# Second attention of a three-stage kernel: scores with the keys on partitions, maxima taken from separate masked scores

## The reference, cut to what matters

```
x = x + xattn(layernorm(x), ctx)      # 16 heads of 16, 4096 keys per batch from ctx
x = x + attn(layernorm(x))            # 16 heads of 16, 256 keys per batch, |i - j| <= 32 only
x = x + ffn(layernorm(x))             # router, 2 of 16 banks per token, 256 -> 1024 -> 256
```

```
qkv = x @ w_qkv + b_qkv
scores = einsum('bhqd,bhkd->bhqk', q, k) / 4 + mask     # mask: 0 within 32 tokens, else -inf
attn = softmax(scores)
out = einsum('bhqk,bhkd->bhqd', attn, v) @ w_out + b_out
```

## Time and profile before

| | us |
|---|---|
| median of 3 runs | 1396.68 (1395.20 to 1401.56) |
| the profiled execution, its own time | 1402.28 |
| its span in the profile | 1400.5 |
| from the copy after the last weighing of the first attention (L964) to the last sum of the second (L1176) | 938.5 to 1116.1 |

### The profile page before, as it was taken

One profiled execution on the slowest core, in us unless ns is written; L12 is line 12 of the kernel. 1 busy time (PEld: TensorE's weight loads), 2 busy tenths in 40 slices (PEclk: granted clock), 3 DMA queues, 4 the chain that ended last, 5 costly groups with the idle time before them and its releaser, 6 DMA issues.

```text
span 1400.5 us, 29968 instructions
## 1 busy us (share of the span) xinstructions
PE 1291.0 (92%) x12251; PEld 800.7 (57%) x12251; DVE 919.1 (66%) x1727; ACT 750.7 (54%) x1043; POOL 270.3 (19%) x244
## 2 busy tenths in 40 slices
PE   7789999999999999999999999988998529999996
PEld 4444444555444455444455544437777429999995
DVE  5778888676888776888767788536677652222224
ACT  4236777676777766777667677844465301111110
POOL 5130212111121211121111111101500011222210
PEclk8989999999999999999999999998999959999998
DMA  7553574533364444357334443100000049999952
GB/s 214 84 74 47 77 162 65 77 54 46 52 134 99 67 69 60 52 105 129 53 52 68 62 61 47 48 8 0 2 1 17 0 158 408 363 333 324 323 195 102
DMA packets 48360, 150.22 MB, mean 107 GB/s; under 512 B 17040, under 2 KB 21152, under 8 KB 40288
## 3 DMA queue, kind: packets, MB, share of 16 engines
q1 hardware_dynamic: 43664, 135.60, 42.1%
q0 software_dynamic: 2976, 8.13, 1.8%
q10 hardware_dynamic: 1584, 4.59, 0.8%
HBM read 88.63 MB, written 6.16 MB: 68 GB/s over the span
## 4 chain that ended last, share of the span: by engine, by line
PE 84%; DVE 8%; ACT 4%; issue 2%; DMA 1%; SPq 0%; DVEq 0%; ACTq 0%
PE psum L546 20%; PE psum L528 14%; PE psum L506 10%; PE psum L844 8%; PE psum L856 8%; PE psum L427 7%; PE psum L444 6%; ACT wts L919 2%; PE psum L715 2%; DVE o_norm L1158 2%; DVE part_max L1116 1%; PE psum L733 1%; PE psum L627 1%; DVE biased L1254 1%; PE psum L574 1%
## 5 line engine op out<-in xcount | busy, mean ns | idle before, releaser
L1116 DVE TENSOR_REDUCE part_max<-psum 128x1 f32<-128x512 f32 x1024 | 656.2, 686 | 180.5 <-PE psum L506 179.1
L919 ACT ACTIVATE wts<-psum 128x1024 f32<-128x1024 f32 x512 | 516.1, 1024 | 96.2 <-PE psum L528 95.2
L546 PE MATMUL psum<-wts,vals 128*17 128x256 f32 x4096 | 319.3, 387 | 0.0
L528 PEld LDWEIGHTS psum<-queries,keys 51*128 51x128 f32 x2048 | 158.3, 186 | 201.9 <-issue 142.6
L528 PE MATMUL psum<-queries,keys 51*128 51x256 f32 x2048 | 260.9, 333 | 7.9 <-ACT wts L919 7.0
L506 PE MATMUL psum<-keys,queries 51*128 51x512 f32 x1024 | 229.9, 444 | 24.9 <-DVE part_max L1116 14.9
L1056 ACT ACTIVATE hid<-psum,b1s 128x128 f32<-128x128 f32 x124 | 35.4, 369 | 207.6 <-PE psum L844 207.6
L546 PEld LDWEIGHTS psum<-wts,vals 128*17 128x17 f32 x4096 | 69.7, 95 | 121.5 <-issue 98.4
L506 PEld LDWEIGHTS psum<-keys,queries 51*128 51x128 f32 x1024 | 97.9, 186 | 42.2 <-DVE part_max L1116 28.3
L844 PE MATMUL psum<-xTt,w1s 128*128 128x128 f32 x992 | 117.7, 278 | 0.2 <-DVE xTt L1436 0.2
L844 PEld LDWEIGHTS psum<-xTt,w1s 128*128 128x128 f32 x992 | 115.1, 194 | 0.6 <-issue 0.6
(11 more groups left out here) (188 smaller groups left out, 1009.3 us busy)
## 6 DMA issues: line engine op xcount, KB each, us to landing
keys<-key_high SPq DMA_DIRECT2D x256, 128.0 KB, 4.4
w1s<-in_W SPq DMA_DIRECT2D x31, 1024.0 KB
w2s<-in_W SPq DMA_DIRECT2D x31, 1024.0 KB
keys<-key_low SPq DMA_DIRECT2D x128, 128.0 KB, 6.1
ctx_in<-in_ctxT SPq DMA_DIRECT2D x12, 768.0 KB, 7.9
ctx_in<-in_ctxT ACTq DMA_DIRECT2D x4, 768.0 KB, 10.7
queries<-query_high SPq DMA_DIRECT2D x64, 32.0 KB, 4.6
queries<-query_low SPq DMA_DIRECT2D x32, 32.0 KB, 4.8
```

The lines of the kernel that those rows point to most:

```text
L528: m = e.matmul(bank(S_BANKS[S_NO["s", n] % 2] + i)[:, hh * SEQ:(hh + 1) * SEQ], keys[64 * i:64 * i + STK, hh, c, at:at + P], queries[g % 3 ...
L546: i = e.matmul(bank(O_BANK)[32 * j:32 * j + VW, 0:SEQ], vals[:, t, h * VW:(h + 1) * VW], wts[n % NW][:, j * SEQ:(j + 1) * SEQ], start=(t = ...
L919: i = e.activation(wts[n % NW], s_bank(job, 2), ACT.Exp, scale=QSCALE)
L1116: e.reduce_max(part_max[g % 2][:, hq, c:c + 1], bank(M_BANKS[n % 3]), AX_X).then_inc(dve_max, 1)
```

## The change

A pair p (one batch, four heads) becomes the unit of the loop; the loop runs over i = 1 to 20 and holds several pairs at different stages. Heads of a group are taken by parity (heads 0, 2, 4, 6 of a half or 1, 3, 5, 7), so that each of the four lies in its own 32 rows with its neighbour set to zero. There are only two masked copies of the queries, written as the projection leaves PSUM (`q_parity`), and no `mask_half`.

- PE `max2(p, qt)`: scores with the queries on partitions, for the maxima only. The mask is put into PSUM first, as a bf16 product of the identity and the mask; then four heads of 32 contraction rows, two at a time in two banks (4 and 5), with a wait between the two twos. DVE takes minus the maximum straight from PSUM.
- DVE `pieces2`: splits it into three bf16 pieces. PE `neg2` turns them (bank 6), ACT `neg_rows` copies them to SBUF as bf16 rows.
- PE `scores2(p)`: mask, scores with the keys on partitions (four heads of 32 rows in banks 0 to 3), and rows of minus the maximum through a weight of ones. ACT `exps` takes exp of 128 x 640 from PSUM, twice a pair; the result is used by `weigh2` as it stands.
- The normalization: ACT copies the spread sums (`sums2`), DVE takes the reciprocal, POOL multiplies and adds the bias.
- The first two `max2` are issued in steps 509 and 511 of the first attention. The projection of the last batch of the first attention is made in one piece at i = 1, instead of twelve instructions at step 512 and four after `last_norm`.
- The second half of transposed rows, queries, keys and values comes in three lumps, at i = 4, 5 and 6, through banks 0 to 3; the copies are shared between ACT and DVE.
- Host-side layouts of w_out, b_v and hmask follow the order by parity.

The diff, cut to its core:

```
-                if n == STEPS:
-                    e.wait_ge(dve_early, 10)
-                    e.wait_ge(pool_norm, LAST)
-                    project_some(wo, range(NG - 1), M_BANKS)
+                if n in FIRST_MAX2:                       # (STEPS - 3, STEPS - 1)
+                    max2(0, FIRST_MAX2.index(n))
...
+            def max2(p, qt):                              # PE
+                ...
+                    e.wait_ge(dve_m2, 2 * p + qt)
+                for odd in range(2):
+                    for i in range(2):
+                        e.matmul(bank(W_BANKS[i])[:, odd * WIN:(odd + 1) * WIN], identb, wmaskb[:, qt],
+                                 start=True, stop=False)
+                    if odd:
+                        e.wait_ge(pe_even2, 2 * p + qt + 1)
+                    for i in range(2):
+                        r = slice(32 * (2 * i + odd), 32 * (2 * i + odd) + 32)
+                        t = e.matmul(bank(W_BANKS[i])[:, odd * WIN:(odd + 1) * WIN], q2[r, par, m, tok:tok + P],
+                                     k2[r, m, keys_at:keys_at + WIN], start=False, stop=True)
+                    t.then_inc((pe_even2, pe_m2)[odd], 1)
+            def neg2(p):                                  # PE
+                e.wait_ge(dve_neg2, p + 1)
+                e.wait_ge(x_free, X_NO["neg2", p])
+                for qt in range(2):
+                    t = e.matmul(bank(X_BANK)[:, qt * P:(qt + 1) * P], neg_parts2[p % 2][:, qt]..., identb, ...)
+            def scores2(p):                               # PE
+                    e.wait_ge(act_w2, 2 * p)
+                ...
+                for h in range(GH):
+                    e.matmul(bank(h)[:, 0:2 * WIN], identb, wmaskb..., start=True, stop=False)
+                for kt in range(2):
+                    for h in range(GH):
+                        e.matmul(bank(h)[:, kt * WIN:(kt + 1) * WIN], k2[r, m, tok:tok + P], q2[r, par, m, at:at + WIN], ...)
+                for kt in range(2):
+                    for h in range(GH):
+                        t = e.matmul(bank(h)[:, kt * WIN:(kt + 1) * WIN], ones2[r], neg_rows2[p % 2][r, at:at + WIN], ...)
+            def weigh2(p, kt):                            # PE
+                for lo, hi, first in (((0, WIN, True),), ((SEQ - WIN, WIN, False), (WIN, SEQ, True)))[kt]:
+                    for h in range(GH):
+                        t = e.matmul(o[32 * h:32 * h + VW, lo:hi], vals2[...], w[:, h, at:at + hi - lo], ...)
...
+            for i in range(1, PAIRS + 5):                 # PE
+                max2(i, 0); weigh2(i - 3, 0); scores2(i - 2); max2(i, 1)
+                weigh2(i - 3, 1); norm2(i - 4); neg2(i - 1)
+                if i == 1: last_project()
+                if i == 4: ... turn_half(1, k, bank(k))
+                if i == 5: ... qk_half(1, m, bank(m))
+                if i == 6: ... v_tile2(TT // 2 + t, bank(t))
+                if i in (8, 12, 16): project2((i - 8) // NG)
+                if i == PAIRS: turn3(0)
+                if i == PAIRS + 1: logits(0); turn3(1)
+                if i == PAIRS + 2: logits(1)
+            for i in range(1, PAIRS + 5):                 # ACT
+                exps(i - 2); ocopy2(i - 3); sums2(i - 4); neg_rows(i - 1)
+                for n in {4: ..., 5: ..., 6: ...}.get(i, ()): half(n)
+            for i in range(1, PAIRS + 5):                 # DVE
+                max2(i, 0); reciprocals2(i - 5); max2(i, 1); pieces2(i)
+                if i == 1: add_last(); statistics(last)
+                if i == 2: root(last); apply(xn2, last, dve_rows2)
+                if i == 5: ... q_parity(1, m, bank(m), dve_half)
+                ...
```

More of the change, by code:

```diff
@@ L601, in project2, with norm2 @@
+            def norm2(p):
+                e.wait_ge(act_ocopy2, p + 1)
+                e.wait_ge(x_free, X_NO["norm2", p])
+                e.matmul(bank(X_BANK)[:, 0:SEQ], lsel, o_raw2[p % 2], start=True, stop=True).then_inc(pe_norm2, 1)
             def project2(b):
[L602 removed]
+                e.wait_ge(pool_norm2, NG * (b + 1))
                 e.wait_ge(x_free, X_NO["out2", b])
@@ L608, in project2, with last_project @@
                 i.then_inc(pe_out2, 1)
+            def last_project():
+                e.wait_ge(pool_norm, LAST)
+                e.wait_ge(dve_lastnorm, 1)
+                e.wait_ge(x_free, X_NO["out"])
+                for qt in range(BT):
+                    for hg in range(NG):
+                        i = e.matmul(bank(X_BANK)[:, qt * EMB:(qt + 1) * EMB], o_norm[:, hg, qt * P:(qt + 1) * P],
+                                     wo[:, hg], start=(hg == 0), stop=(hg == NG - 1))
+                i.then_inc(pe_lastout, 1)
             def project_some(w, groups, to):
@@ new lines, in _ @@
+            for i in range(1, PAIRS + 5):
+                if i < PAIRS:
+                    max2(i, 0)
+                if 0 <= i - 3 < PAIRS:
+                    weigh2(i - 3, 0)
+                if 0 <= i - 2 < PAIRS:
+                    scores2(i - 2)
+                if i < PAIRS:
+                    max2(i, 1)
+                if 0 <= i - 3 < PAIRS:
+                    weigh2(i - 3, 1)
+                if 0 <= i - 4 < PAIRS:
+                    norm2(i - 4)
+                if i - 1 < PAIRS:
+                    neg2(i - 1)
+                if i == 1:
+                    last_project()
+                if i == 4:
+                    e.wait_ge(act_w2, 2 * (i - 1))
+                    for k in range(KE):
+                        turn_half(1, k, bank(k)).then_inc(pe_half, 1)
+                if i == 5:
+                    e.wait_ge(act_w2, 2 * (i - 1))
+                    for m in range(2 * KE):
+                        qk_half(1, m, bank(m)).then_inc(pe_half, 1)
+                if i == 6:
+                    e.wait_ge(act_w2, 2 * (i - 1))
+                    for t in range(TT // 2):
+                        v_tile2(TT // 2 + t, bank(t)).then_inc(pe_half, 1)
+                if i >= 8 and i % NG == 0 and (i - 8) // NG < BATCH - 1:
+                    project2((i - 8) // NG)
+                if i == PAIRS:
+                    turn3(0)
+                if i == PAIRS + 1:
+                    logits(0)
+                    turn3(1)
+                if i == PAIRS + 2:
+                    logits(1)
```

472 lines of the change are left out of this document (224 added, 248 removed).

## The result

The changed kernel takes 1381.5 us (median; 1375.8 to 1383.2) beside 1397.5 of the kernel before on the same chip: a ratio of 0.9875, interval 0.9838 to 0.9912. It is faster by 16 us between the medians and by 1.25% by the ratio, and the interval is clear of no change. Forecast was 1372, faster, in a range of 1352 to 1398. Sign and range hold; the gain is 16 us instead of 25. Its profiled execution took 1381.6 by its own time, 20.7 less than that of before.

The account below looks back on a forecast made before the run. PE's instruction stream was taken to set the pace, 6.45 us a pair; stage terms 0.4 + 22.9 + 77.4 + 12.2 + 8.2 + 1 + 30.3 = 152.4 us against 177.6 gave 1377 profiled, 1372 median; range 1352 to 1398.

Parts of the forecast that it names:

- TensorE's stream sets the pace, and how long it is for a pair: Steady iteration: PE's instructions for a pair take 5.9 us, plus waits at neg2, a period of 6.45; before 7.3.
- Its terms: PE's stream per pair: max2 twice 2.8 us, scores2 1.55, weigh2 1.0, norm2 0.43, neg2 0.11.
- A change of division: Switching how PE's array is divided between products: 0.25 us each, ends 0.20 and about 0.45; 12 a pair, 192 in all.
- The rival of dear changes: Changes of the array's division cost more: gain gone at 0.38 us each, 1405 at 0.42; chance 0.13.
- Four sets of rows abreast: 32-row products on PE overlap four at a time, 0.033 us each; rival of overlap two by two, 1383, chance 0.14.
- The end of the first attention at nothing: Before the stage: two max2 add 2.8 us, the leaving L614 block saves 2.86, so no net effect.
- The start, 22.9 and 0.4: Stage's beginning, i = 1 to 3: 22.9 us after a copy of 0.4.
- The twelve iterations with lumps and two projections: i = 4 to 15: iterations 77.4 us, lumps 12.2, two projections 8.2, VectorE's statistics 1.
- The end, 30.3: From i = 16 to the last addition: third projection done at 8.9 us, POOL at 26.9, last projection and addition at 30.3.
- The offset: Whole kernel: 1377 for the profiled execution, lowered to 1372 because the profiled execution before stood 5.6 above its median.
- the clock: Rival: PE at 1.2 GHz in a third of the stage, +20 to +45 us, 1405 to 1420; chance 0.04 shared with no overlap.
- the copies out of PSUM gave nothing by going: Stage: removed copies of the turned weights lie beside PE already, so the sum credits their removal with nothing.

Follow-up runs that it names:

- run 1: Changed kernel with neg2 of the pair before moved right behind its first max2, and its ScalarE copy to the iteration's head; 1376.4 us, ratio 0.981.
- run 2: Changed kernel with three 128-row products of zeros a pair added in scores2, so six more changes of the array's division a pair; 1393.6 us, ratio 0.9945.
- run 3: The control: changed kernel with the same added products of zeros in scores2, but through 32 rows, so no added change of division; 1381.5 us, ratio 0.9864.
- run 6: Changed kernel with the mask products of max2 left out, maxima over all 160 keys; 1375.9 us, ratio 0.9839.
- run 5: Changed kernel with filler products only, in TensorE's long waits at i = 1, before neg2 of i = 16 and before the last projection; 1375.4 us, ratio 0.9838.
- run 7: Changed kernel with one mask product of 320 columns per bank in max2 instead of one of 160 per group; 1382.8 us, ratio 0.9898.
- run 9: run 8 plus filler products in TensorE's remaining waits, at i = 3, 4 and 16 to 18, behind the third projection and router products; 1364.7 us, ratio 0.9755.
- run 8: Changed kernel with neg2 early, twelve instructions of the first attention's last projection moved into the gap at i = 1, and some fillers; 1370.8 us, ratio 0.9791.
- 10: run 9 with the mask products of max2 left out as well, fillers kept; 1354.6 us, ratio 0.9683.
- 11: Same kernel as 10 (neg2 early, projection in the gap, no max2 masks) without any filler; 1358.7 us, ratio 0.9716.

## Why the prediction was right, and where it was off

- **TensorE's stream sets the pace, and how long it is for a pair**: right. 6.56 for 6.45, and run 1 confirms the wait of 0.57 by removing it: 6.02. That the sum came so near is in part luck, as the next point shows.
- **Its terms**: right only in their sums. A change of division was taken as 0.25, by the distance to a product that follows another; it is 0.11 by itself (runs 2 and 3, and run 6) for changes between 32-row and 128-row products, the only pairing tested. Three errors made up for it. In max2 the wait between the even and the odd groups was to fall into a change; it is 0.34 and longer than one. In scores2 the four masks were set at 0.40, though the price of 0.067 for 160 columns makes them 0.53, and 0.65 lies between the first of the sixteen products and the next block, not 0.53. And a max2 by the prediction's own prices (masks 0.13 and products 0.13, both twice, and four changes of 0.25) is 1.52, not 1.4. With these two sums put right the period would have come out at about 6.8. The rival of dear changes, given a chance of 0.13, is refuted: it needed 0.38.
- **Four sets of rows abreast**: right. In run 2 each half of the products, eight instructions, takes 0.49 to the next block with a change in it; at 0.033 each they are 0.27, and two by two 0.53 without any change. In the control eight take 0.38 (1023.19 to 1023.57) and in the changed kernel sixteen 0.65, so eight more add 0.27. By the Trainium skill's factor of 3.07 ("TensorE: Matmul & The Clock Gate", Measured speedup vs the span model), which is stated for 512 columns, the sixteen would take 0.69, an estimate; the 0.65 with what stands behind the last is under it.
- **The end of the first attention at nothing**: the copy is at 938.99, before at 938.53. That neither confirms nor refutes it, since kernels with the same instructions reach that copy anywhere from 931.9 to 939.0.
- **The start, 22.9 and 0.4**: this step failed. max2(4, 0) starts 25.25 behind the copy, 1.95 late. The wait behind last_norm was in the sum, 2.2 us; that everything behind it, max2(1, 1) and sixteen projections, ran at 1.2 GHz was not: 1.0 and 1.5 us, a little of it given back by VectorE's work alongside. Run 5, with that wait filled, confirms it: 22.65 us, 2.6 less, and 0.65 under the sum's 23.3.
- **The twelve iterations with lumps and two projections**: 98.74 by the trace (964.24 to 1062.98), 98.8 by the sum, but by errors that cancel. Twelve periods of 6.56 are 78.7, 1.3 over; the three lumps took 11.3 for 12.2 and the two projections 8.5 for 8.2; of the 1 us for VectorE's statistics 0.2 is left.
- **The end, 30.3**: the same step again. The last projection starts 26.84 behind max2's place in i = 16 (1062.98 to 1089.82), for 26.9, but this is luck. The third projection ended 11.2 behind that place and not 8.9, with 1.7 of the 2.3 us by its low clock (5.38 for 3.69), and the profile's chain of work that ended last runs through the whole of it. What made up for it is that the rest up to L708 took 15.65 us, for 18.0. Then L708, behind its 3.4 us of waiting, took 5.45, and with the addition 5.98 (to 1095.80) instead of 3.4. Of these 2.6 us the clock is 1.8; at full clock in run 5 the same two take 4.14, so 3.4 was 0.7 too low by itself.
- **The offset**: the sum gave 1377 for the profiled execution, and 1381.6 was measured, 4.5 over. The stage has 4.4 of them (156.8 for 152.4): 1.95 at the start and 2.6 at the end. The other 5 us of the miss in the median are the 5.6 that I took off for the profiled execution of before. That was a run at a clock of 0.965, while runs of before in the later sets reach 0.972, and there was no reason for the changed kernel's profiled run to stand off its own median; it did not.
- **Rivals**: the clock stood there with 0.04 together with another, as a third of the stage at 1.2 GHz. It should have been a term of the sum: small in this kernel (7.8 us by 156.8 at 0.95, about what the stage before has, 177.6 at 0.95), and up to 29 us in those that take work off TensorE (run 6; but run 2, which adds work, has 25). The price written there slips too: 20 to 45 us on 1372 are 1392 to 1417, not 1405 to 1420. That the copies out of PSUM gave nothing by going is not shown. No run takes them alone away, and in the kernel before TensorE did wait for them between 950 and 1120, ten times and 9.0 us in all, 0.19 at a time in the dense part (at 1029.89 and at 1037.21) and 4.0 once:

```profile
PE psum L728 <- ACT wTa L1018: 9.0, 10, 4.0
```

So of the 25 us expected in the stage 20.8 came in the profiled executions. Nothing was lost in the steady part and 4.5 us went at both ends. The low clock cost more than that there, 2.6 us at the start (run 5), 1.7 and 1.8 at the two projections of the end; smaller terms of the sum that were too high hid the rest. The main step that went wrong is one: everything behind a long wait of TensorE was priced at the full clock. It made the gain smaller, not the direction wrong.

## What to carry to other kernels

Work the steady iteration out by distances between starts and the round trip of one bank, and it can come out to 2%, as here, partly by errors that cancel: check each term, and not only the sum. Then ask of every wait of TensorE what the granted clock does behind it. Behind 2.1 to 3.4 us it fell every time here, behind 0.3 to 1 us in some executions. Taking work off TensorE can leave it waiting, and a clock of 0.5 for 20 us eats the gain: move real work into the waits first, then filler products, and compare kernels at the same granted clock before a change is called useless. Compare the stage that the change touches, too: what lies ahead of it varied by 7 us from one execution to the next. Profiled execution and median differ by the clock of that one run, so take no offset over from one kernel to another.

## What the runs showed of the hardware that I had not expected

- The clock stayed at 1.2 GHz for 20 us and more while TensorE was busy (4.00 of 4 us at 0.50 in run 1), once it had fallen behind a wait of 0.93 us.
- Behind the same wait of 0.71 us the clock fell at once in three executions (runs 2, 3 and 7) and not in two (the changed kernel and run 5).
- With products that compute nothing in waits of 0.5 to 0.6 us it was at 2.4 GHz for 110 us (run 9; without them, in run 8, it fell there). Over the span the clock was 0.969 to 0.972 in every run with fillers and 0.962 to 0.966 in every run without (10 and 11).
- A change of the array's division between 32-row and 128-row products costs 0.11 us; a semaphore between two groups that write the same banks 0.34, three times as much.
